# First tile loads that wait for batch 3's scatters only where they must, and batch 3's last gate and up block behind the expert loop

## What is computed

```python
# cross attention: every batch by itself
q = ctx @ Wq.T + bq;  k = ctx @ Wk.T + bk                  # 4 x 512 x 128
att = softmax(q @ k.T)                                     # 512 x 512 per batch
x = x + tanh(g_xattn) * mix(layernorm(x), att)
# feed forward over all 2048 rows, 8 experts of inner width 352, the best two taken
flat = layernorm(x).reshape(2048, 512)
shared = (sigmoid(flat @ sg.T) * (flat @ su.T)) @ sd.T     # float32, for every row
w, idx = top_k(softmax(flat @ router.T), 2)
routed = sum over the 2 chosen e of w * ((sigmoid(flat @ wg[e].T) * (flat @ wu[e].T)) @ wd[e].T)   # bfloat16
x = x + tanh(g_ffn) * (flat + shared + routed)
```

## Time and profile before

| what | us |
|---|---|
| median of 3 runs | 313.82 |
| lowest and highest | 312.88 and 317.53 |
| the profiled execution's own time | 314.28 |
| its span, first to last instruction | 312.5 |

### The profile page before, as it was taken

The page is one execution under the profiler, slowest core; times in us unless marked ns, Lnnn a source line. Parts: engine busy times, 40 slices in busy tenths (PEclk is TensorE's granted clock), DMA queues, the critical chain, the costliest instruction groups (busy, mean ns, idle before and its releaser), DMA issues.

```text
span 312.5 us, 5663 instructions
## 1 busy us (share of the span) xinstructions
PE 293.0 (94%) x1607; PEld 208.1 (67%) x1607; DVE 209.7 (67%) x578; ACT 133.3 (43%) x238; POOL 140.2 (45%) x163
## 2 busy tenths in 40 slices
PE   7979779999999999999999999999999999999980
PEld 2558558786877767787887787666666666665720
DVE  0578878477847458776883886577676777766093
ACT  2573677604658642733724722333433333342000
POOL 3708892584900581292279073034434344344100
PEclk9999899999999999999999999999999999999996
DMA  6999899021170021004965992334343343449597
GB/s 208 397 253 312 149 211 302 32 85 36 67 269 0 9 86 42 0 2 71 210 158 113 205 197 80 101 94 128 104 124 116 119 122 103 132 97 313 168 382 290
DMA packets 30492, 46.01 MB, mean 147 GB/s; under 512 B 2880, under 2 KB 20032, under 8 KB 30464
## 3 DMA queue, kind: packets, MB, share of 16 engines
q1 hardware_dynamic: 19888, 27.66, 28.3%
q0 software_dynamic: 10432, 17.99, 25.0%
q10 hardware_dynamic: 144, 0.00, 0.0%
HBM read 39.58 MB, written 14.72 MB: 174 GB/s over the span
## 4 chain that ended last, share of the span: by engine, by line
PE 72%; issue 8%; POOL 6%; DVE 5%; DMA 3%; ACT 3%; SPq 0%; DVEq 0%; POOLq 0%; ACTq 0%
PE bank L763 15%; PE bank L495 12%; PE bank L497 11%; PE bank L496 11%; PE bank L780 8%; POOL xg L430 5%; PE bank L490 4%; PE bank L753 3%; PE bank L510 3%; PE bank L771 2%; DMA wqk_sb<-wqk 1%; ACT prob L861 1%; DMA xg<-lnb,slot 1%; POOL hT_lo L419 1%; DMA xt<-xg 1%
## 5 line engine op out<-in xcount | busy, mean ns | idle before, releaser
L479 POOL DMA_INDIRECT z<-ysb,dest x39 | 37.2, 955 | 62.4 <-DVE ysb L1420 62.1
L1031 ACT ACTIVATE sigc<-bank 128x352 f32<-128x352 f32 x39 | 18.1, 463 | 54.3 <-PE bank L763 54.3
L1415 DVE TENSOR_TENSOR hrow<-sigc,bank 128x352 bf16<-128x352 f32 x39 | 20.3, 521 | 24.0 <-ACT sigc L1031 24.0
L430 POOL DMA_INDIRECT xg<-lnb,slot x32 | 31.7, 991 | 9.9 <-issue 7.3
L763 PE MATMUL bank<-wgu_lo,xTb 128*128 x156 | 36.0, 313 | 0.0
L763 PE MATMUL bank<-wgu_hi,xTb 128*128 x156 | 36.0, 313 | 0.0
L780 PE MATMUL bank<-wd_sb,hTb 128*128 (+1 forms) x117 | 31.8, 381 | 0.1
L495 PE MATMUL bank<-lnT_hi,sgu_lo 128*128 128x512 f32 (+2 forms) x72 | 29.6, 411 | 1.6 <-DVE lnT_lo L1127 1.6
L1420 DVE TENSOR_SCALAR ysb<-bank,wt 128x512 bf16<-128x512 f32 x39 | 29.1, 746 | 1.0 <-PE bank L780 0.9
L497 PE MATMUL bank<-lnT_hi,sgu_hi 128*128 128x512 f32 (+2 forms) x72 | 28.4, 394 | 0.0
L496 PE MATMUL bank<-lnT_lo,sgu_hi 128*128 128x512 f32 (+2 forms) x72 | 28.3, 394 | 0.0
(11 more groups left out here) (192 smaller groups left out, 646.4 us busy)
## 6 DMA issues: line engine op xcount, KB each, us to landing
xt<-xg SPq DMA_DIRECT2D x39, 129.0 KB
xT_raw<-xT SPq DMA_DIRECT2D x4, 1024.0 KB, 7.4
acc<-x SPq DMA_DIRECT2D x4, 1024.0 KB, 10.0
out<-acc SPq DMA_DIRECT2D x16, 256.0 KB, 3.7
wgu_lo<-wguT POOLq DMA_DIRECT2D x2, 1408.0 KB, 13.4
wgu_hi<-wguT POOLq DMA_DIRECT2D x2, 1408.0 KB, 13.4
cx<-ctxT SPq DMA_DIRECT2D x4, 512.0 KB, 6.4
wd_sb<-wdT POOLq DMA_DIRECT2D x2, 1024.0 KB, 10.6
```

Of the source, the lines that this page charges most:

```text
L430: nc.gpsimd.indirect_dma_start(out=xg, out_offset=bass.IndirectOffsetOnAxis(ap=slot[:, c, j:j + 1], axis=0), in_=lnb[c][:, j, :], in_offse ...
L479: nc.gpsimd.indirect_dma_start(out=z, out_offset=bass.IndirectOffsetOnAxis(ap=dest[:, u:u + 1], axis=0), in_=ysb[:, r, :], in_offset=None) ...
L1031: act.activation(sigc[:, v, :], bank[2 * v][:, 0:I], ACT.Sigmoid).then_inc(s["csig"], 1)
L1415: V.tensor_tensor(hrow[:, v, 0:I], sigc[:, v, :], bank[2 * v + 1][:, 0:I], ALU.mult).then_inc(s["ch"], 1)
```

## The change

The first four tile loads. Batch 3's eight scatters now count on a semaphore of their own, `scat_end`. GpSimd waits for them all and raises `all_rows` from 1 to 2. VectorE works out after `tables_rows` for each of the first four tiles whether it holds rows of batch 3 (`late_i` is 2) or not (1). SyncE waits for the 24 scatters of batches 0 to 2, for `tabs` and for `late`, then reads four row numbers and four of these values into registers, and then waits for each of the first four loads until `all_rows` has reached its value. All later loads wait for 2. `lnb` and `ysb` now share memory, so the first result waits for `all_rows` 2 as well; `lgT` and `hTb` share memory too.

The block. `wide_shared(3, 2, 0)` and `(3, 2, 1)`, with `gate_shared`, `shared_hidden`, `hidden_high` and `hidden_low` of that block, stand behind the loop, in banks 4 and 5. `rows_in(0)` comes before `down(2, 3)`. In VectorE's program `shared_out(2, 3)`, `hidden_low(3, 0)` and `(3, 1)` come behind `rows_out(0)`. The `down` of batch 3 is split in two parts of six and three matmuls a row block, laid between the `routed` ones.

```diff
@@ block.sync
-            sp.wait_ge(s["scat"], 16 * TOP * TT)
+            sp.wait_ge(s["scat"], 16 * TOP * LT * last_b)
             sp.wait_ge(s["tabs"], 1)
+            sp.wait_ge(s["late"], 1)
             sp.wait_ge(s["t2"], TT)
...
+            first = [sp.value_load(erow[0:1, r:r + 1], min_val=0, max_val=E * REG) for r in range(SLOTS)]
+            whose = [sp.value_load(late_i[0:1, r:r + 1], min_val=1, max_val=2) for r in range(SLOTS)]
             for r in range(SLOTS):
-                load_tile(r, r, None)
+                sp.wait_ge(s["all_rows"], whose[r])
+                sp.dma_start(xt[:, r, :], xg[bass.ds(first[r], P), :]).then_inc(s_xl[r], 16)
+            sp.wait_ge(s["all_rows"], 2)
@@ block.gpsimd
             scatter(last_b, 0)
             scatter(last_b, 1)
+            pool.wait_ge(s["scat_end"], 16 * TOP * LT)
+            nc.gpsimd.memset(mark[:], 0.0).then_inc(s["all_rows"], 1)
@@ block.tensor
-            for j in range(LT):
+            for j in range(LT - 1):
                 down(b, j)
...
-            wide_shared(last_b, 2, 0)
-            wide_shared(last_b, 2, 1, range(0, 2))
             rows_in(0, 0, 0)
-            wide_shared(last_b, 2, 1, range(2, NT))
+            down(b, LT - 1)
             pe.wait_ge(s["hid"], IT * last_b + 2)
-            pe.wait_ge(s["sigd"], IT * NB)
...
-            for j in (2, 3, 0, 1):
-                down(last_b, j)
-            for t in range(LT * last_b):
+            wide_shared(last_b, 2, 0)
+            wide_shared(last_b, 2, 1)
+            down(last_b, 0, (0, 1))
+            down(last_b, 1, (0, 1))
+            for t in range(4):
                 routed(t)
-            for j in range(LT):
+            down(last_b, 2, (0, 1))
+            for t in range(4, 7):
+                routed(t)
+            down(last_b, 3, (0, 1))
+            for t in range(7, 10):
+                routed(t)
+            down(last_b, 0, (2,))
+            for t in range(10, LT * last_b):
+                routed(t)
+            routed_last(0)
+            for j in range(1, LT):
+                down(last_b, j, (2,))
                 routed_last(j)
@@ block.vector
+            def tables_late():
+                added = upto[:, :, LT - 1]
+                link(V.tensor_tensor(over[:], tf[:], limit[:], ALU.subtract))
+                link(V.tensor_tensor(late_in[:], added[:, 1:E], added[:, 0:E - 1], ALU.subtract))
+                link(V.tensor_tensor(late_of[:], start[:, 0:SLOTS, 0:E - 1],
+                                     late_in[:].rearrange("p (a e) -> p a e", a=1).to_broadcast([P, SLOTS, E - 1]), ALU.mult))
+                link(V.tensor_reduce(late[:], late_of[:], AX.X, ALU.add))
+                link(V.scalar_tensor_tensor(out=late[:], in0=over[:, 0:SLOTS], scalar=0.0, in1=late[:], op0=ALU.min, op1=ALU.add))
+                link(V.tensor_scalar(late[:], late[:], added[:, 0:1], 0.0, ALU.add, ALU.is_gt))
+                V.tensor_scalar(late_i[:], late[:], 1.0, None, ALU.add).then_inc(s["late"], 1)
...
             tables_rows()
+            tables_late()
...
             rows_out(0, 0)
-            shared_hidden(last_b, 2)
+            shared_out(b, 3)
+            hidden_low(last_b, 0)
+            hidden_low(last_b, 1)
             step(0, 0)
-            hidden_low(last_b, 2)
...
+            shared_hidden(last_b, 2)
+            hidden_low(last_b, 2)
             for t in range(LT * last_b):
                 add_routed(t)
```

54 lines of the change are left out of this document (35 added, 19 removed).

## The result

The changed kernel is slower by 1.1%. Its median over 20 runs is 318.38 us (316.16 to 319.73), that of the kernel before 314.61 (312.77 to 317.53) in 20 runs beside them; the ratio is 1.0115, with a 95% interval of 1.0087 to 1.0143. The execution that was profiled took 317.49 us, with a span of 315.6, against 314.28 and 312.5. The forecast was 316.6, with a range of 312.8 to 319.6.

What follows compares the result with a forecast made beforehand. TensorE was taken to bound the kernel (busy 94% of the span), VectorE the tail after `down`. On 314.28 us, −0.55 (earlier tile) + 1.2 (half clock) + 1.7 (tail) = +2.35 gave 316.6, range 312.8 to 319.6.

Steps and rivals of the forecast that it cites:

- `late` at 186.2: Loop's start, VectorE: seven small chained operations from 184.65 on have `late` ready at 186.2.
- Eight register loads in 4.6 us: Loop's start, SyncE: eight serial register loads take 4.6 us, so the first DMA starts at 191.1.
- From T to the second gate and up, 5.5 at full clock: Loop's start: from the first tile's landing T (193.15) to the second tile's gate and up, 5.5 us before any clock loss.
- The half clock: Loop's start: TensorE's longer idle gap halves its clock when `down(2, 3)` starts; +1.2 us, bounds 0 and +2.0.
- Rival (b): Loop's start: the clock stays full, or is full again before `down(2, 3)`; 315.4 us, chance 0.20.
- Rival (c): Clock at half well into the loop's first tiles, and last store as late as before; 318.9 us, chance 0.12.
- GpSimd and tile 3 at nothing: Loop's start: three tiles go early, tile 3 waits, lands near 196, needed near 200; GpSimd's wait delays nothing; no cost.
- rival (d): Loop's start: the first tile is taken for late too, its DMA starting at about 193.1; 318.6 us, chance 0.05.
- Rival (a): Loop's start: faster register loads, first tile landing at 190.7 at the least, turning point 192.05; 313.0 us, chance 0.13.
- The tail at +1.7: After the loop: 24 more matmuls make TensorE set the end, +2.2 us, less 0.5 for stores; +1.7 us.
- The term on the additions: Tail: `routed(0)` 8.57 after the loop, last addition ending 13.45 after that instead of 11.27; +2.2 us.
- The term on the stores: Tail: stores come slower, so the last may land sooner; 0 to −1.1 us, taken as −0.5.

Runs made afterwards that it cites:

- the filler: Changed kernel plus twenty matmuls nobody reads in TensorE's gap ahead of the first tile's transposes; 1.001.
- `tables_sent` moved: Changed kernel with row number and bound read per tile just ahead of its DMA, and VectorE's `tables_sent` behind the loop's sixth tile; 0.9891.
- the second series: Four kernels run beside the kernel before, among them the changed kernel again with no edit; that one measured 1.005, median 315.99 us.
- the block's move alone: Changed kernel, but all four first loads wait for all scatters, with one register load ahead of each; 1.0134, and 1.0113 when run again.
- the loads in pairs: Changed kernel, but SyncE reads each tile's row number and `late_i` value just ahead of its DMA; 0.9888.
- one load: Changed kernel, but each tile reads only its row number and the bounds on `all_rows` are constants; 0.9895.
- The store experiment: Kernel before the change with the stores of the first eight row blocks of `out` left out; 0.9943.
- the third series: Four kernels run beside the kernel before, among them the changed kernel again with no edit; that one measured 1.0035.

## Why the prediction was right, and where it was not

The forecast's kind was right, no difference of 2% and a small loss, and the range held the median; 318.38 lies 1.8 us above the 316.6. Its own range of the likeliest case (315.4 to 318) holds the medians of the two later series of the changed kernel (315.99 and 315.43), and not that of the first 20 runs. The mechanism at the loop's start was right. The total was close in part by luck, as the sum below shows.

**The place of the loss: right.** SyncE's register loads end last ahead of the first DMA, TensorE stands idle for it, `down(2, 3)` is late behind it, and `shared_out(2, 3)` and the low parts behind that. Shown by the chain of waits, and by undoing one link at a time: with the loads shortened the kernel is at 0.9895, with `down(2, 3)` moved forward at 0.9992.

**`late` at 186.2: right.** It stands 1.63 after the start of `erow` (187.17 less 185.54); forecast were 1.67.

**Eight register loads in 4.6 us: too small.** This is the term that was off most. From the first load to the first DMA the forecast had 4.9. The changed kernel's executions have 4.95, 5.6 and 6.7. The four loads of the earlier trace rows had durations of mostly 0.27; in the execution with 5.6 the median over the four reads of `erow` is 0.47. In the one with 6.7 there are besides five pieces of about 0.7 in the chain, which no other execution has. The Trainium skill (DMA: Bandwidth & Descriptors, section Latency and other measured facts) gives a floor of about 600 ns a load; by it eight take 4.8. From the first load to the last check the three traces have 4.75, 5.4 and 6.5, that is 0.59, 0.68 and 0.81 for each. So the floor fits the shortest of the three, the two others lie above it, and the 0.57 read from the earlier trace rows lies below all of them. The first DMA was forecast 6.57 from `erow` and comes at 8.48: 1.9 of the 2.3 us by which the loop's start was missed; 1.8 are the loads, and 0.1 the step from `late` to the first of them, which the sum had at nothing.

**From T to the second gate and up, 5.5 at full clock: right.** With the filler 5.4, with `tables_sent` moved 5.4.

**The half clock: right in kind, 1.5 instead of 1.2.** In the profiled execution it falls during the idle time (192 to 194) and lasts through most of `down(2, 3)`; in the repeat of the second series it falls soon after T (1.00 from 192 to 194, 0.55 from 194 to 196) and lasts to the end of `down(2, 3)`. The filler took it away. Rival (b), a full clock, is out: three executions of the changed kernel have the fall. Rival (c) had 318.9, near the median of the first 20 runs, by a longer half clock and late stores. Neither is in the three traces of the changed kernel. Its clock part is in both traces of the block's move alone, where the half clock reaches the first tile's gate and up. And the executions at that median had a lower clock than the profiled one (0.978 against 0.984). So for them (c)'s clock is not ruled out: no trace shows where they ran at half.

**GpSimd and tile 3 at nothing: right.** With the loads in pairs the first three DMAs start at 188.81, 190.60 and 192.55, GpSimd's mark comes at 194.94, and the fourth DMA at 195.21. So tiles 0 to 2 went early and tile 3 waited: the first tile was not taken as late and rival (d) is out. One price was not in the sum: where the tiles really go early, the last scatter takes longer (3.50 with one load, 2.92 in the earlier trace rows); no run shows that it delays the loop. Rival (a), fast register loads, is out too. The kernels with one load or two ahead of the first DMA are its case made true by an edit, and they show what it brings: 310 to 311, a larger gain than its 313.0, since the tile then stands 4.9 to 5.5 from `erow` (190.7 was 6.2), and neither a half clock nor a dearer tail takes from it.

**The tail at +1.7: too large.** The term on the additions was right to a tenth: `routed(0)` 8.53 behind the loop (8.57 forecast) and the last addition's end 13.51 behind that (13.45). The term on the stores was mis-sized: the last store now lands 2.2 after its issue instead of 4.7, so relief is 2.5 in this trace and 1.5 in those with a tail of 25.7, where it lands after 3.2 or 3.3, not 0.5. Net, the tail is 24.5 to 25.7 in the nine other traces that have the tail of the change whole, against 25.05 and 24.27 in the two traces with the old one: between −0.5 and +1.5, and +0.4 by the two means. I had read the tail as VectorE's "without a gap" from the earlier trace rows. The store experiment shows that the last thing in it was the DMA engines' queue, and the earlier trace rows had the hint: two stores in a row with landings of 3.6 and 4.7, where each lands in 2.2 once half of them are left out.

**The sum.** Against the profiled execution the forecast had +2.35: +0.65 at the loop's start and +1.7 in the tail. The trace has 2.91 at the start, −0.49 in the loop and −0.33 in the tail. Two mis-sized terms of opposite sign, and an execution that began 1.0 late, make up a total that looked better than its parts; that much was luck. (Rival (a)'s 192.05 should read 192.0; nothing hangs on it.)

**What stays open.** Why the register loads take 4.95 in one execution and 6.7 in another was not tried. Nor was why the ratio of the same kernel is 1.0115 in the first 20 runs, 1.005 in the second series and 1.0035 in the third. The length of the loads in the trace goes the same way (6.7, 4.95, 5.6) only in its largest value. The granted clock goes with it: its mean over the executions was 0.980 in the first 20 runs and 0.987 in both later series. Of the 26 executions of the kernel before in the third series those at 0.981 or 0.982 took 314.4 to 315.9, those at 0.991 to 0.993 took 312.6 to 313.5, so 0.010 of clock goes with 2 us. By that 0.007 is some 1.4 us, an estimate, of the 2.4 to 3.0 by which the medians of one kernel differ. What made the clock lower in the first 20 runs stays open.

## What to carry to other kernels

SyncE's register loads were serial here, and each cost 0.6 to 0.8 us: read just ahead of a transfer only what that transfer needs, and let the other reads wait behind it; that edit alone turned 1.0035 to 1.0115 into 0.989. Work that fills a wait belongs ahead of the waiting instruction, and where a cover is taken away, something that was cheap (a wait, a clock) gets a price. Before a tail is called an engine's, look at how long its last stores take to land: where they queued, 2.2 us of extra work ahead of the last of them cost between −0.5 and +1.5.

## What the runs showed that I had not expected

The DMA engines bound the last microseconds of the kernel before. At one store of 262 kB each 0.66 us, with 401 GB/s moved, the landing time rose to 4.7; with half of the stores left out it was 2.1 to 2.3 throughout, and the kernel 0.6% faster, although VectorE's last addition ended no earlier.

The granted clock fell after rather little idle time. In the kernel with `down(2, 3)` moved forward TensorE idled 2.72 us, and the windows show:

```profile
194.00:196.00 2.00, 0.95 (x9) 0.79 (x10) 0.92 (x4) 0.00 (x0) 0.00 (x0) 0.78 0.65 182
196.00:198.00 2.00, 2.00 (x9) 1.03 (x7) 0.56 (x3) 0.00 (x0) 0.00 (x0) 0.50 0.31 70
```

It came to 0.50 only after TensorE was at work again, as in the earlier trace rows, and from T to the second gate and up it took 4.3, where the kernel before took 3.55 (195.65 to 199.20). The kernel was still no slower, since its tile came 1.6 earlier from `erow` (9.53 and 11.12).

And the start of `erow`, in code that all kernels share, lay between 183.85 and 186.39 over the fourteen traces of this study. A comparison of two single traces by absolute times would have put up to 2.5 us of that down to the edits. What goes with it is the granted clock in the first 50 us, which stands at 0.50 for none, one or two short stretches there. The one trace with none (the block's move alone, third series) has `erow` at 183.85; the four with one between 36 and 41 us, the kernel before among them, at 184.08 to 184.56; the six with one between 17 and 23, the changed kernel among them, at 184.74 to 185.60; the three with two at 186.26 to 186.39. That orders all fourteen; no run was made to test it.
